# A fused attention and ternary-weight layer: third-last batch's codes turned by the DMA, its product and its scaling placed later

## The reference

```python
# x, f: (16, 256, 256) float32; itok: (16,) stage of each batch
bias = braak_embed[itok][..., None]
attn = softmax(einsum('bsd,btd->bst', x + bias, f), axis=-1)
y = einsum('bst,btd->bsd', attn, f)

xh = y @ H                                   # H: 256x256 Hadamard / 16
scale = clip(max(abs(xh), axis=-1), 1e-5) / 7
xq = clip(round(xh / scale), -8, 7) * scale

w_scale = clip(mean(abs(weight), axis=1), 1e-5)
wq = where(weight / w_scale > 0.5, 1, where(weight / w_scale < -0.5, -1, 0)) * w_scale
out = x + einsum('bsi,oi->bso', xq, wq)
```

## Time and profile before

| | us |
|---|---|
| median of 3 runs (lowest to highest) | 105.21 (105.18 to 105.61) |
| the profiled execution | 105.24 |
| its span, from the first to the last record of the trace | 103.4 |
| PE busy | 96.7 (94%) |
| DVE busy | 86.7 (84%) |
| ACT busy | 77.1 (75%) |
| POOL busy | 47.9 (46%) |
| granted TensorE clock, mean, as a share of full speed | 0.992 |

### The profile page before, as it was taken

One profiled execution on the slowest core, in us unless ns is written; L12 is line 12 of the kernel. 1 busy time (PEld: TensorE's weight loads), 2 busy tenths in 40 slices (PEclk: granted clock), 3 DMA queues, 4 the chain that ended last, 5 costly groups with the idle time before them and its releaser, 6 DMA issues.

```text
span 103.4 us, 2603 instructions
## 1 busy us (share of the span) xinstructions
PE 96.7 (94%) x799; PEld 90.6 (88%) x799; DVE 86.7 (84%) x223; ACT 77.1 (75%) x201; POOL 47.9 (46%) x70
## 2 busy tenths in 40 slices
PE   5999899999999999999999999999999999999640
PEld 2449799999999999999999999999999999899420
DVE  1084789698989999899989898989999998988881
ACT  3265986969697878787878969697878784786820
POOL 5034699604343435454544445343535454504880
PEclk9999999999999999999999999999999999999996
DMA  2994740536236572879283645647382122221126
GB/s 59 237 321 132 209 189 3 206 51 203 54 107 198 166 230 73 255 66 292 51 273 82 236 119 172 183 121 234 107 235 76 46 57 88 51 101 42 59 101 203
DMA packets 14850, 14.71 MB, mean 142 GB/s; under 512 B 8054, under 2 KB 8956, under 8 KB 14844
## 3 DMA queue, kind: packets, MB, share of 16 engines
q1 hardware_dynamic: 14400, 14.36, 47.0%
q10 hardware_dynamic: 444, 0.28, 0.9%
HBM read 8.73 MB, written 4.19 MB: 125 GB/s over the span
## 4 chain that ended last, share of the span: by engine, by line
PE 81%; DVE 8%; DMA 3%; ACT 3%; issue 2%; ACTq 1%; DVEq 0%
PE score_bank L477 19%; PE xh_bank L477 19%; PE fh_bank L477 14%; PE prob_bank L466 7%; PE f_bank L466 6%; PE q_bank L466 6%; PE out_bank L535 6%; DMA stage_of<-itok_dram 3%; ACT prob L696 2%; DVE xh_bank L1027 1%; DVE last_result L1033 1%; DVE abs_max L1007 1%; PE q_bank L477 1%; PE f_bank L477 1%; DVE abs_max L995 1%
## 5 line engine op out<-in xcount | busy, mean ns | idle before, releaser
L356 POOL TENSOR_TENSOR result<-scaled,x_all 128x512 f32<-128x512 f32 x13 | 16.7, 1283 | 20.8 <-DVE scaled L870 20.2
L348 POOL TENSOR_TENSOR code<-code,magic 128x512 bf16<-128x512 f32 x13 | 13.5, 1042 | 12.5 <-ACT code L674 12.5
L690 ACT CAST fh_hi<-fh_bank 128x512 fp32r<-128x512 f32 x16 | 9.4, 588 | 8.3 <-PE fh_bank L477 8.3
L696 ACT ACTIVATE prob<-score_bank,neg_max 128x256 f32<-128x256 f32 x30 | 14.0, 478 | 0.6 <-DVE neg_max L913 0.5
L477 PE MATMUL fh_bank<-had,f_hi 128*128 128x256 f32 x64 | 14.0, 299 | 0.0
L884 DVE TENSOR_TENSOR prob_lo<-prob_bank,prob_hi 128x512 fp32r<-128x512 f32 x16 | 11.1, 691 | 3.5 <-ACT prob_hi L686 3.5
L477 PE MATMUL score_bank<-f_hi,q_hi 128*128 128x256 f32 x60 | 13.2, 302 | 0.0
L665 ACT CAST f_hi<-f_bank 128x512 fp32r<-128x512 f32 x15 | 8.8, 587 | 5.7 <-PE f_bank L466 5.6
L674 ACT ACTIVATE code<-xh_bank,inv_scale 128x256 f32<-128x256 f32 x30 | 12.7, 482 | 0.3 <-DVE inv_scale L867 0.2
L477 PE MATMUL fh_bank<-had,f_lo 128*128 128x256 f32 x64 | 12.7, 281 | 0.0
L884 DVE TENSOR_TENSOR f_lo<-f_bank,f_hi 128x512 fp32r<-128x512 f32 x15 | 10.3, 688 | 2.2 <-ACT f_hi L665 2.2
(11 more groups left out here) (149 smaller groups left out, 236.4 us busy)
## 6 DMA issues: line engine op xcount, KB each, us to landing
f_nat<-f_dram SPq DMA_DIRECT2D x16, 256.0 KB, 2.7
x_all<-x_dram SPq DMA_DIRECT2D x16, 256.0 KB, 3.0
out_dram<-result SPq DMA_DIRECT2D x14, 256.0 KB, 2.0
w_raw<-weight_dram SPq DMA_DIRECT2D x1, 256.0 KB, 4.8
out_dram<-result SPq DMA_DIRECT2D x2, 128.0 KB, 1.8
out_dram<-last_result ACTq DMA_DIRECT2D x2, 128.0 KB, 1.8
code_t<-code SPq DMA_TRANSPOSE x13, 2.5
had_block<-hadamard_dram SPq DMA_DIRECT2D x1, 64.0 KB, 3.8
```

The source lines that it names most:

```text
L348: nc.gpsimd.tensor_tensor(as_rows(code16[:, b.k]), as_rows(code), magic[:, :].broadcast_to([P, W]), ALU.subtract).then_inc(code16_ready, 1)
L356: nc.gpsimd.tensor_tensor(result[:, b.k], as_rows(scaled[:, b.k]), x_all[:, b.at], ALU.add).then_inc(result_ready, 1)
L690: nc.scalar.copy(fh_hi[:, b.k], fh_bank[:, :, :]).then_inc(fh_hi_ready, 1)
L696: a = nc.scalar.activation(prob[:, t], score_bank[:, t], ACT.Exp, bias=neg_max[:, b.k, t:t + 1], accum_out=row_sum[:, b.k, t:t + 1])
```

## The change

The count of batches whose codes the DMA turns rises from 13 to 14, so that the third-last batch is among them. That adds on POOL its conversion, and on SP the transposing DMA (through turned_by_dma in SP's loop); it drops turn_code(third_last) on PE and decode(third_last) on ACT. The ternary product of the third-last batch moves on PE from ahead of the last batch's mixing to between its two tiles, and waits for the DMA's semaphore code_turned. On ACT the quantising of the second-last batch moves ahead of the scaling of the third-last product. The semaphore counts that depend on turned_by_dma shift by one with it.

```diff
-        turned_by_dma = B - 3
+        turned_by_dma = B - 2
...
             third_last, second_last, last = (Batch(0, B - n) for n in (3, 2, 1))
+
+            pool.wait_ge(code_ready, third_last.at + 1)
+            pool.wait_ge(code_turned[third_last.k], 16 * third_last.half)
+            nc.gpsimd.tensor_tensor(
+                as_rows(code16[:, third_last.k]), as_rows(code), magic[:, :].broadcast_to([P, W]),
+                ALU.subtract).then_inc(code16_ready, 1)
 
             for b in (second_last, last):
...
             times_ternary(fourth_last)
             times_hadamard(last)
-            turn_code(third_last)
             turn_prob(last)
             mix(second_last)
-            pe.wait_ge(prob_ready, B)
-            pe.wait_ge(code_t_ready, third_last.at + 1 - turned_by_dma)
-            for t in range(T):
-                mm = ternary_tile(third_last_out_bank, t, third_last)
-            mm.then_inc(third_last_out_in_bank, 1)
             pe.wait_ge(prob_hi_ready, B)
             pe.wait_ge(fh_lo_ready, B)
             for t in range(T):
                 product(last_xh_banks[t], mixed(last), [t],
                         wait_for_last_part=lambda: pe.wait_ge(prob_lo_ready, B)
                         ).then_inc(last_xh_in_bank, 1)
+                if t == 0:
+                    pe.wait_ge(code_turned[third_last.k], 16 * third_last.half + 16)
+                    for u in range(T):
+                        mm = ternary_tile(third_last_out_bank, u, third_last)
+                    mm.then_inc(third_last_out_in_bank, 1)
...
             split_prob(last)
-            decode(third_last)
+            quantize(second_last)
 
             act.wait_ge(third_last_out_in_bank, 1)
...
             a.then_inc(third_last_scaled, 1)
-            quantize(second_last)
             for t in range(T):
```

## The result

| | before | changed |
|---|---|---|
| median of the runs taken together, us | 105.19 (105.08 to 105.61, 4 runs) | 107.42 (106.33 to 108.15, 4 runs) |
| the profiled execution | 105.24 | 107.00 |
| its span | 103.4 | 105.2 |

The changed kernel takes 1.0157 times as long, with a 95% interval of 1.0102 to 1.0213. It is slower, as forecast, but the median lies above the range of 105.95 to 106.8. Its four runs are 106.33, 107.00, 107.84 and 108.15.

The account below looks back on a forecast made before the run. PE, busy 94%, was taken to bound the steady loop, and a chain through PE and then DVE the tail. Scaling later by 1.50, less POOL's slack of 0.41, plus 0.08 at the stores gave +1.17: 106.4 us, range 105.95 to 106.8.

Parts of the forecast that it names:

- What comes off PE: PE's tail: dropping four transposes of the third-last codes saves 0.24, moving the second-last maximum on DVE up by 0.24.
- the product's later place: PE's tail: the third-last ternary product, 0.36, is only moved behind the last batch's first tile; worth nothing.
- The transposing DMA: POOL, SP, PE: issued at 92.40, landed at 94.90, wanted at 95.18; costs nothing while the 0.28 margin holds.
- The rival of a late landing: Transposition lands at the longest, 4.0, making POOL's chain 0.28 later: +1.45, 106.7; chance 0.10.
- ACT's order and POOL's queue: ACT's third-last scaling ends 1.50 later; less POOL's slack of 0.41, DVE's last four instructions are late by 1.09.
- the 0.6 to 1.0 asked for: Sign to look for: DVE waiting 0.6 to 1.0 for POOL's last output scale before its first last-batch scaling.
- The rival that POOL does not decide: POOL's chain shorter or its scale needed later; only 0.10 of ACT's later quantising left: 105.3, no change; chance 0.08.
- the one that the cut on PE reaches the end: Rival: DVE's whole chain comes 0.24 earlier, giving 105.0; chance 0.04.
- The stores: End of the span: last stores queue at 0.44 each (297 GB/s), the last ending at 103.77; queue adds 0.08.
- The sum: Whole kernel: scaling later by 1.50, less POOL's slack of 0.41, plus 0.08 at the stores: +1.17, giving 106.4.

Follow-up runs that it names:

- scaling_first: Changed kernel with ACT's old order put back, third-last product scaled ahead of the second-last quantising; 106.39 us, ratio 1.0093 to the kernel before.
- quantise_first_only: Kernel before with only the second-last quantising moved ahead of the third-last scaling on ACT; 106.57 us, ratio 1.0107.
- tilewise: Changed kernel with the third-last scaling and POOL's work on it cut in tiles, last output scale between the tiles; 105.44 us, ratio 1.0012 to the kernel before.
- after_padded: Changed kernel with eight long-fulfilled waits more on SP at the start; 106.50 us, ratio 1.0094 to the kernel before.
- late_load: Changed kernel with the load of the stage numbers held back until the first batch's f has landed; 110.83 us, ratio 1.0492 to the kernel before.
- before_three_waits: Kernel before with three long-fulfilled waits more on SP at the start; 106.18 us, ratio 1.0068.
- output_scale_first: Changed kernel with POOL making the last batch's output scale ahead of its two third-last instructions; 106.20 us, ratio 1.0071 to the kernel before.

## Why the prediction was right or wrong

The times of the changed kernel are put on the clock of the kernel before by taking off 0.70.

| step | forecast | measured |
|---|---|---|
| second-last maximum on DVE earlier by | 0.24 | 0.24 (from the fourth-last product 3.69, then 3.45) |
| transposition issued | 92.40 | 92.37 |
| third-last product on PE, no wait | 95.18 | 95.09 |
| ACT quantises the second-last | 95.98 | 95.97 |
| ACT scales the third-last, from, to | 96.77, 97.61 | 96.70, 97.54 |
| POOL starts L420 | 97.71 | 97.62 |
| POOL starts the last output scale | 100.29 | 100.20 |
| DVE starts the last batch | 100.53 | 100.42 |
| DVE ends | 102.32 | 102.23 |
| last store's data ends | 103.77 | 103.6 |
| tail and store together | +1.17 | +1.10 |

**What comes off PE: right.** The whole 0.24 reached the maximum. That the product's later place is worth nothing held only because ACT quantises first; in ACT's old order it delays ACT by 0.46 (scaling_first).

**The transposing DMA: right.** The issue on SP and the landing times in the changed kernel, and PE's product without a wait:

```profile
93.07 1.20 SPq L288 DMA_TRANSPOSE code_t<-code  x1
...
DMA to landing us min/median/max: 2.4/2.5/3.8
```

```profile
95.79 0.61 PE L541 MATMUL score_bank<-tern_t,code_t 128*128 128x256 bf16 x4
```

The rival of a late landing did not come about: the tails of the changed kernel's profiles are 11.10 to 11.12.

**ACT's order and POOL's queue: right, and shown by two experiments.** The wait is there at 0.85, within the 0.6 to 1.0 asked for, and the move of one call does it (quantise_first_only) or undoes it (scaling_first). The chain was forecast 0.09 too late at its end, nearly all of it because ACT went from the quantising to the scaling in 0.73 (96.67 to 97.40) and not in 0.79. The rival that POOL does not decide is out. So is the one that the cut on PE reaches the end, for this kernel; tilewise has it reach DVE's end by 0.20, and then the stores keep it.

**The stores: the size came out by luck.** The forecast had the queue add 0.08, and the store is 0.10 longer. But the queue added nothing. The busy share of the DMA engines in slices of 0.025, from 101.7 in the kernel before and from 103.4 in the changed one:

```profile
DMA  9797979998999853391959896989897864611000
```

```profile
DMA  9899999999999988794989999998989873901000
```

The last packets are in the slices to 102.63 and to 104.33, 1.40 behind DVE's end in both. The last 9 of the second line is the fetch of instructions, with one packet of the store behind it. With the fetch moved away (after_padded) the store is 2.16, as before, so the 0.10 goes with the fetch, for which the step had no term. That this was only 0.1 in the changed kernel is luck too: three waits on SP put 0.7 on the kernel before. The rate itself was as in the earlier trace rows, 296 GB/s over the last stores of the changed kernel:

```profile
102.60:104.40 1.80, 0.00 (x0) 0.00 (x0) 0.33 (x1) 0.00 (x0) 0.00 (x0) 0.50 0.89 296
```

By the Trainium skill (DMA: Bandwidth & Descriptors, section "Where 436 GB/s comes from"), with its limit of about 358 GB/s, there would have been no queue. No run here shows that rate over the last stores, so that there was no queue does not confirm this reckoning.

**The sum and the range: wrong.** The step that failed is "The sum": how the +1.17 was laid on the runs. It took the median of three runs within 0.43 of each other as firm, added +1.17, and built the range from doubts about the tail alone. There was no term for when the stage load lands, although the trace of before has a wait of 3.85 for it at the start, with all of PE behind it. In the profiled execution it put 0.70 on the span with the tail as forecast: 1.8 is 0.70 + 1.00 + 0.10. And there was none for the executions that are 1 to 2 above the others, of which the four runs had two. These two carry the median out of the range. Their cause stays open: a late stage load with a slow PE behind it fits (late_load), but no trace of such a run exists. The eleven lower of the changed kernel's sixteen runs have their median at 106.61. The kernel before, over the sittings of the experiments, has 105.40 without its thirteen upper runs. Their difference of 1.21 is close to the forecast's +1.17, in part by luck, since the traces have 1.00 for the tail and 0.10 for the store, the latter from the fetch. And a median of four runs of which any may fall in the upper group needed a range up to 107.5 or more.

## What to carry to other kernels

Where an instruction is moved back on one engine, follow its result to the engine that waits for it, and there ask what small but urgent instruction stands behind it; its slack (0.41 here), not that of the result itself, sets the price. Where two edits come together, try each alone, and do not expect their effects to add up: the move on ACT alone cost 1.23 of the tail, the rest alone cost 0.16, and both together 1.00. Before a difference under 1 us is put down to an edit, look whether an instruction fetch has moved into the last store, and whether the start of the two profiles is the same.

## What the runs showed of the hardware that was not expected

An instruction fetch (one packet of queue q14) moves over the DMA engines that also carry the stores. Where it fell into the last 128 KB store (at 102.6 in scaling_first, 102.2 in before_three_waits), nine of that store's packets came 0.4 to 0.9 behind the rest, and the span ended 0.8 to 0.9 later (2.94 and 3.11 against 2.16 and 2.17). Where it fell among the very last packets (the changed kernel, tilewise, output_scale_first), at most one packet stands behind it. Three fulfilled waits on SP were enough to bring that about.

PE, idle for 3.03 ahead of q_bank in late_load, ran its pairs of products at 0.43 instead of 0.24 for some 4 us, while the granted clock of those rows read 1.00. Idle times of 0.20 to 1.30 at the same place had no such effect. So at the start of a program the durations must be looked at, not the clock's column alone.
